# Products of a zero tile in TensorE's gaps, from the kernel's start to the scores of the first pair

## The reference, cut to what matters

```
xn   = layer_norm(x, norm1_g, norm1_b)                 # over 128 channels
xw   = windows of 8 x 8 of roll(xn, (-4, -4))          # 64 windows of 64 tokens
qkv  = xw @ qkv_w.T + qkv_b                            # 16 heads of 8
q, k = rope2d(q), rope2d(k)
attn = softmax(q @ k.T * 8**-0.5 + attn_mask)          # 64 x 64 per head and window
x    = x + unroll(attn @ v @ proj_w.T + proj_b)
h    = layer_norm(x, norm2_g, norm2_b) @ fc1_w.T + fc1_b
x    = x + (silu(gate) * a) @ fc2_w.T + fc2_b          # a, gate = halves of h
f, g, v = x @ Wq + bq, x @ Wk + bk, x @ Wv + bv        # layer 1, per image: 1024 tokens
out  = gamma * softmax(f @ g.T) @ v + x
```

## Time and profile before

| what | value |
|---|---|
| median of 3 runs | 393.1 us |
| lowest and highest run | 390.09 and 394.24 us |
| the profiled execution's own time | 393.27 us |
| its span, first to last instruction | 391.5 us |
| mean granted clock of TensorE in the span | 0.983 |
| busy share PE / DVE / ACT / POOL | 90 / 77 / 70 / 70 % |
| share of PE in the chain that ended last | 60 % |

### The profile page before, as it was taken

One profiled execution on the slowest core, in us unless ns is written; L12 is line 12 of the kernel. 1 busy time (PEld: TensorE's weight loads), 2 busy tenths in 40 slices (PEclk: granted clock), 3 DMA queues, 4 the chain that ended last, 5 costly groups with the idle time before them and its releaser, 6 DMA issues.

```text
span 391.5 us, 12541 instructions
## 1 busy us (share of the span) xinstructions
PE 350.5 (90%) x4900; PEld 229.4 (59%) x4900; DVE 300.3 (77%) x818; ACT 273.9 (70%) x447; POOL 274.8 (70%) x326
## 2 busy tenths in 40 slices
PE   2668999899999999998979989999997999999993
PEld 0334665555666666665746655566555675767673
DVE  6758988788888888889785668787766778697433
ACT  2466988887877788887664365443567788878892
POOL 7476966677777677799565867766536687788842
PEclk9999999999999999999699999999999999999998
DMA  6701100111011011110000010000010102010012
GB/s 195 242 22 29 30 22 22 31 29 30 23 32 32 26 27 28 29 29 17 2 3 2 0 28 2 2 1 3 2 26 3 29 2 67 15 40 18 22 35 59
DMA packets 15596, 12.29 MB, mean 31 GB/s; under 512 B 3991, under 2 KB 14136, under 8 KB 15544
## 3 DMA queue, kind: packets, MB, share of 16 engines
q1 hardware_dynamic: 14208, 11.03, 9.8%
q10 hardware_dynamic: 1336, 0.54, 0.5%
HBM read 4.22 MB, written 2.10 MB: 16 GB/s over the span
## 4 chain that ended last, share of the span: by engine, by line
PE 60%; DVE 17%; ACT 5%; DMA 5%; issue 5%; SPq 3%; POOL 3%; POOLq 0%; ACTq 0%; DVEq 0%
PE ps L359 8%; PE ps L1580 7%; PE ps L911 6%; DMA k_t<-qk_t 5%; PE ps L939 5%; PE ps L993 4%; PE ps L932 4%; PE ps L901 3%; PE ps L920 3%; SPq L871 3%; PE ps L379 3%; PE ps L903 2%; DVE mx L1676 2%; PE ps L1422 2%; PE ps L375 2%
## 5 line engine op out<-in xcount | busy, mean ns | idle before, releaser
L1297 POOL TENSOR_TENSOR p_lo<-e_buf,p_hi 128x1024 f16<-128x1024 f32 x32 | 68.2, 2131 | 6.7 <-ACT p_hi L1153 4.7
L1787 POOL TENSOR_TENSOR el<-e,eh 128x1024 f16<-128x1024 f32 x28 | 59.6, 2132 | 17.6 <-ACT eh L1766 17.3
L1289 POOL TENSOR_TENSOR rot<-ta,tb 128x256 f32<-128x256 f32 x32 | 23.3, 728 | 38.0 <-DVE tb L1084 37.2
L359 PE MATMUL ps<-y_t,fc_w 128*128 128x512 f16 x192 | 46.2, 380 | 2.5 <-DVE hid L532 1.1
L1111 DVE TENSOR_REDUCE ps<-ps 128x16 f32<-128x1024 f32 x32 | 39.4, 1233 | 7.4 <-PE ps L920 6.5
L911 PE MATMUL ps<-mask,identb 128*128 128x512 bf16 x128 | 39.8, 393 | 6.0 <-DMA k_t<-qk_t 5.9
L1223 ACT ACTIVATE e_buf<-ps 128x1024 f32<-128x1024 f32 x32 | 32.7, 1023 | 14.5 <-PE ps L932 14.3
L288 POOL TENSOR_TENSOR hl<-hid,hh 128x512 f16<-128x512 f32 x24 | 27.6, 1157 | 19.7 <-DVE yn L569 10.6
L1580 PE MATMUL ps<-val,eh 128*128 128x129 f16 x512 | 36.5, 220 | 2.2 <-DVE ob L1710 1.6
L1580 PEld LDWEIGHTS ps<-val,eh 128*128 128x128 f16 x512 | 31.2, 98 | 12.0 <-issue 8.8
L1755 ACT ACTIVATE e<-ps 128x1024 f32<-128x1024 f32 x32 | 32.6, 1020 | 7.9 <-PE ps L1569 7.6
(11 more groups left out here) (166 smaller groups left out, 1005.4 us busy)
## 6 DMA issues: line engine op xcount, KB each, us to landing
k_t<-qk_t SPq DMA_DIRECT2D x126, 32.0 KB, 1.9
x_all<-in_x SPq DMA_DIRECT2D x8, 256.0 KB, 4.5
out<-ob SPq DMA_DIRECT2D x8, 192.0 KB, 2.1
yr<-xr SPq DMA_DIRECT2D x16, 64.0 KB, 2.0
mask_f<-in_mask SPq DMA_DIRECT2D x1, 512.0 KB, 3.8
fc_w<-in_fc_w SPq DMA_DIRECT2D x1, 512.0 KB, 5.9
out<-ob SPq DMA_DIRECT2D x4, 128.0 KB, 2.1
fc_w<-in_fc_w SPq DMA_DIRECT2D x1, 256.0 KB, 5.6
```

Source lines behind the costliest of these rows:

```text
L359: last = pe.matmul(ps[:, bank, :], fc1_w16[:, ws, 128 * block_:128 * block_ + 128], y_t[:, v, ys, :], start=(n == 0), stop=(n == 2))
L1297: pool.tensor_tensor(p_lo[:, u], e_buf[:, u], p_hi[:, u], ALU.subtract).then_inc(plo_done, 1)
L1787: pool.tensor_tensor(el[:, T % H_BUFS, :], e4[:, T % E_BUFS, :], eh[:, T % H_BUFS, :], ALU.subtract).then_inc(el_done, 1)
```

## The change

A tile `zeros` of 128 x 512 in 16-bit floats is added, which DVE clears first of all. A function `keep_busy(count)` on TensorE multiplies it with itself `count` times into bank 6; nobody reads the results, and the products signal nobody. It is called in five places: 16 products before the first real product, 8 after the turn of chunk 0, 6 ahead of the first turn of step -1, 3 ahead of that of step 0, and 8 ahead of the wait for the mask and the keys of pair 0. That makes 41 products. The only new wait is TensorE's for the cleared tile.

```diff
+        zeros = sb("zeros", [128, CHUNK], F16)
+        zeros_set = sem("zeros_set")
...
+                def keep_busy(count):
+
+                    for k in range(count):
+                        pe.matmul(ps[:, T2_BANK, :], zeros[:, 0:128], zeros[:], start=True, stop=True)
+
+                pe.wait_ge(zeros_set, 1)
+                keep_busy(16)
                 pe.wait_ge(gains_loaded, 16)
                 pe.wait_ge(qkv_loaded, 32)
...
                 ln_turn(0)
+                keep_busy(8)
                 pe.wait_ge(const_loaded, 16)
...
+                    if at_step(n, -1):
+                        keep_busy(6)
+                    if at_step(n, 0):
+                        keep_busy(3)
                     if valid(n, -1):
                         wait(pe, lo_done, n + 2)
...
                         if at_step(n, 0):
+                            keep_busy(8)
                             pe.wait_ge(mask_lo if parts > 1 else mask_hi, 1)
...
             def _(dve):
 
+                dve.memset(zeros[:].bitcast(F32), 0.0).then_inc(zeros_set, 1)
                 for rows in (k_rows[:], q_rows[:]):
```

## The result

The changed kernel took 395.51 us (median of 20 runs, 393.31 to 397.44) against 393.39 us for the kernel before (median of 20, 390.09 to 397.37). The ratio is 1.0067, with a 95% interval of 1.0044 to 1.0089. A ratio, like the two means compared further down, leaves out executions that took over 1.5% more than the fastest of the same kernel, so it isn't the quotient of the two medians. By the ratio the change made the kernel slower by 2.6 us, by the medians 2.1 us; the forecast, 391.6, was about 1.6 us less than before, and 395.51 lies outside its range of 389.6 to 394.2. A later set of runs gave 1.0024 (0.9989 to 1.0060) for the same kernel, so the size is less sure than the first interval says.

The account below looks back on a forecast made before the run. It took a chain of waits without spare time, with TensorE at 1.2 GHz for the first 30 us, as the bound. Gains limited by ACT to -1.6 us gave 391.7 or 391.5, stated as 391.6 us, range 389.6 to 394.2.

Parts of the forecast that it names:

- Memset, and the price and fit of the blocks: At the start: memset costs nothing, a product 0.425 us slow or at most 0.25 fast, and all five blocks fit.
- (a): First projection, 11.20 to 12.34 us: 0.54 instead of 1.14 at the upper clock level, -0.60, passed whole to the keys.
- (b): Masks and scores of pair 0: 1.17 us instead of 2.02 at the upper level, -0.85, in all -1.45.
- (c): Six TensorE pieces from 25.43 to 29.84 us run faster; the maximum of pair 1 starts 2.35 us earlier.
- The first rival: Clock falls again after pair 0's scores; pair 1 gains 1.15 us instead of 2.35; time 392.1 us, chance 0.28.
- The step that failed: After chunk 2's low part on DVE: the -1.6 us left there is carried unchanged to the kernel's end.
- The second rival: Gain given back waiting for keys or at stage seams, where alignment costs or brings 1 to 2 us; 393.2, chance 0.15.
- lucky twin: Favourable alignment, with a clock fall such as that at 203.8 us gone; time 390.0 us, chance 0.08.
- The third rival: Products of zeros don't raise the clock, so every block runs at 0.425 us per product; 399.1 us, chance 0.05.

Follow-up runs that it names:

- f4: The changed kernel's 41 long products plus 87 of 2 columns, 256 added instructions in all, against the kernel before: 392.72 us, ratio 0.9983.
- g3: The changed kernel itself measured once more, on a third chip, against the kernel before: 393.81 us, ratio 1.0024.
- g4: The same kernel as f4 again, on a third chip, against the kernel before: 391.97 us, ratio 0.9982.
- e4: Of the 41 products only the eight ahead of pair 0's scores stay, no padding, against the kernel before: 392.79 us, ratio 1.0021.
- g2: Only the eight long products ahead of pair 0's scores, plus 120 small ones, 256 added instructions, against the kernel before: 392.55 us, ratio 0.9996.
- g1: The 41 long products, 15 more in steps 0 and 2, and 72 small ones, 256 added instructions, against the kernel before: 392.53 us, ratio 0.9989.
- the padded version: The kernel of f4 and g4, 41 long and 87 small products, against the kernel before: 392.72 and 391.97 us, ratios 0.9983 and 0.9982.
- e1: The kernel before, unedited, against itself: 393.84 us, ratio 0.9993.

## Why the prediction was wrong

*Memset, and the price and fit of the blocks: right.* The clock rose inside the sixteen, DVE had no wait from its memset, and no block delayed a real product. The rise came at 4.3 us, earlier than the 6.2 assumed. L887 waited at 7.25 for its load, not for the sixteen.

*The first projection, (a): -0.60.* It took 0.72 us in the chain against 1.14, and rotation began 0.40 earlier. *Masks and scores of pair 0, (b): -1.45 in all.* They took 1.1 us, near the 1.17 forecast, but the keys were no earlier, so the maximum of pair 0 gained 0.89. The prediction passed (a) whole through "the key DMA of 2.92 us, whose durations don't change": the turned keys were copied and sent 0.40 us earlier, and the last transfer took 3.3 us. What made it longer isn't shown. A load of a second instruction queue, q14, starts at 20.0 to 20.1 us in both profiles and may be part of it.

*The stretch from 25 us, (c).* The first rival came true: the clock fell at 24.8, in the place that it named, and the maximum of pair 1 stood at 28.71 (the rival said 28.7) and 1.15 us early, as it said. That it fits to the hundredth is luck: its turn started at 26.09 and not at 25.85. In f4, g3 and g4 the fall is at 24.9 to 25.6 as well. It isn't there in e4 and g2, where the rise came at 21 to 22 us, nor in g1, whose gap was filled. In g1 the forecast held in part. ACT was through with the high part of chunk 2 at 29.76, where 29.9 was forecast, and DVE's low part of it started at 29.84 in place of 31.48: -1.64. But DVE didn't wait for ACT there. The maximum of pair 1 came at 28.23, not at 27.5, since pair 0's keys were late and DVE's own work followed from there, so the size is right and the path to it only nearly.

**The step that failed is the last: "All later waits are on other instructions of the same pipeline, with nothing tied to an absolute time ..., so I carry it to the end."** Two things are tied to neither the work nor the gain. TensorE's program comes in blocks, by loads that run beside the keys' transfers. The 82 new instructions moved every later block's load, which costs about 1.1 us where it meets a key transfer on the chain: 1.1 us from pair 28 to 30 and 0.8 from pair 17 to 19 in both profiles of the changed kernel, and 0.6 and 1.5 in the store at the end. The second rival had the place (keys that come late) and a price of 1 to 2 us, but called it a matter of chance. The loss from pair 28 to 30 goes by the instruction count, and came back in both profiles. The prediction had counted the added instructions as nothing but their duration.

The other thing is the clock, behind the pairs. In the profile of the changed kernel 3.40 us are lost over the span: 1.70 by pair 31 (the start's -1.15, the fall at 38.5 and the two places above among them), 1.65 by the fall at 304.7, 0.59 in the last store, less 0.54 between. The prediction had counted on the kernel before as it was profiled, and that had 10.2 us at the lower level between 186 and 209 us, worth up to 3.8; only the lucky twin of its second rival reckoned with that.

How much each of the two is worth in the medians is known only roughly. Over its 20 and 12 runs the changed kernel's mean clock is 0.978 and 0.981, the padded version's 0.983 and 0.985. Worked out as above, the changed kernel spends 4 us more at the lower level than the padded one. By the slopes of the single runs, 0.3 us each, that is 1.2 of the 2.75 us between them; by the steps behind pair 31, about 0.5 us each, it is 2. The rest, 0.7 to 1.5, goes to the loads. These are estimates, and single profiles scatter about them: by pair 31 the changed kernel is 1.97 us behind the padded one in the first pair of profiles (against f4) and 0.30 in the second (g3 against g4), while the clock makes 4.9 and 3.9 us behind it, and the last store 0.7 and 1.6. Why the clock falls more often in the one than in the other is open, and it isn't shown that the products do it: the unchanged kernel has a fall at 39.1 in e1's profile, and its executions differ among themselves. So is why the first set gave 1.0067 and the later one 1.0024, which is 1.65 us lower in the mean.

Was the early clock worth anything? With the loads back in place, the kernel with all 41 products is at 0.9983 and 0.9982, and both intervals hold 1. In the profiles 0.9 us is gained at pair 2 and 0.1 to 0.2 left at pair 30; the span is 4.2 and 4.3 us shorter than that of the kernel before, but 3.8 us of that are the clock between 186 and 209 us. The ratios agree with the rival's -1.15 and can't be told from no change. No version was measured that surely beats the kernel before. The third rival, that zeros don't raise the clock, is disproved by the rise at 4.3 us.

## What to carry to other kernels

Before you price an edit that only adds instructions, look at the DMA part of the profile for a queue of kind "instruction", and ask what transfers its loads meet now and will meet then. To test an edit for what it computes, pad it to a whole block of instructions, and compare positions in the two traces piece by piece: a loss that sits at one place in profile after profile isn't scatter, even where the medians can't tell. Take the comparison to the last instruction, not to the end of the stage that you changed. A gain at the start of a pipeline that waits for small DMAs is only the start's until a position near the end confirms it.

## What the runs showed of the hardware

- A 16 KB load of TensorE's program beside a 32 KB key transfer: on the chain of waits 1.84 to 1.87 us became 2.43 to 3.81, and an issue on SP's queue of 0.59 us became 1.45 and 1.60. Beside the last store, of 128 KB: 2.1 to 2.4 us became 2.9 to 4.1.
- Products of a zero tile raise TensorE's clock: the rise came at 4.3 us, after products without a pause from 1.2. With eight of them at 19.26, close behind real products, it came at 21.1; without any, at 30.0.
- The windows print a granted clock of 1.00 until the first rise on record, at 30.0 us in the kernel before, though its products until then have durations of the lower level, 1.2 GHz.
- A single execution of one unchanged kernel varied from 389.3 to 397.8 us, and its time went with that at the lower clock, by 0.3 to 0.4 us per us. In the profiles 3.4 us at the lower level cost 1.65 us behind a fall at 301 to 305 us, and 10.2 us cost 3.8 between 186 and 209.
- A product of 2 columns with its weight load took about 0.03 us in a row (56 in 1.66 us).
